# First group's maxima between the last projection products, and layer 1's projections mixed with base and adapter products, in a two-layer transformer kernel

## The reference, cut to what matters

```python
x = L0_attn_x                                   # (2, 1024, 512) f32
xn = _layernorm(x)
x = x + attn0(xn) + ffn0(xn)                    # 32 heads of 16, one k/v head, biases; SwiGLU 512 -> 1376
xn = _layernorm(x)
x = x + attn1(xn) + ffn1(xn)                    # 32 heads, 8 k/v heads, rotary, causal; base + routed adapters
# attn:  Q, K, V = xn @ Wq, xn @ Wk, xn @ Wv ;  softmax(Q K^T / 4) V @ Wo
# ffn1:  xn @ W_base.T + b_base + 2 * sum over the top 2 of 8 experts of gate * (xn @ A_e.T) @ B_e.T   (rank 16)
```

## Time and profile before

| | us |
|---|---|
| median of 3 runs | 2045.32 (2042.33 to 2059.11) |
| the profiled execution | 2046.85, of which its span is 2045.3 |
| layer 0: feed-forward, until | 389.9 |
| layer 0: 20 projection products | 389.9 to 461.5 |
| layer 0: group 0's 23 items alone | 464.3 to 492.8 |
| layer 0: attention and output | 492.8 to 1250 |
| layer 1: base and adapter products | 1274.0 to 1345.2 |
| layer 1: 20 projection products | 1346.1 to 1415 |
| layer 1: V products | 1414.8 to 1443.6 |
| layer 1: group 0's 33 items alone | 1444.4 to 1470.1 |

### The profile page before, as it was taken

One profiled execution on the slowest core, in us unless ns is written; L12 is line 12 of the kernel. 1 busy time (PEld: TensorE's weight loads), 2 busy tenths in 40 slices (PEclk: granted clock), 3 DMA queues, 4 the chain that ended last, 5 costly groups with the idle time before them and its releaser, 6 DMA issues.

```text
span 2045.3 us, 29252 instructions
## 1 busy us (share of the span) xinstructions
PE 1932.7 (94%) x10864; PEld 973.7 (48%) x10864; DVE 1405.1 (69%) x1879; ACT 1094.6 (54%) x2177; POOL 233.4 (11%) x606
## 2 busy tenths in 40 slices
PE   6999999998999999999999999997899999999998
PEld 5888887633333333333333357443433333333436
DVE  6554545328999999999988736369677777777643
ACT  3221211232887887878777743024176666767562
POOL 1000000000000100001000000000124334232230
PEclk9999999996999999999999999998699999999799
DMA  6010100141222112211121001014212121221102
GB/s 207 1 47 1 43 1 1 33 143 41 45 42 61 32 32 42 44 30 31 32 56 30 8 21 38 0 31 120 62 29 47 31 51 29 48 46 31 28 10 86
DMA packets 79212, 87.53 MB, mean 43 GB/s; under 512 B 19072, under 2 KB 52864, under 8 KB 79072
## 3 DMA queue, kind: packets, MB, share of 16 engines
q1 hardware_dynamic: 79072, 85.67, 16.8%
HBM read 55.20 MB, written 20.71 MB: 37 GB/s over the span
## 4 chain that ended last, share of the span: by engine, by line
PE 79%; DVE 9%; ACT 7%; issue 2%; SPq 1%; DMA 1%; POOL 0%; DVEq 0%; POOLq 0%
PE ps L1373 19%; PE ps L1403 11%; PE ps L1088 7%; PE ps L1089 7%; PE ps L1090 7%; ACT arena L738 6%; PE ps L1399 6%; PE ps L1320 6%; PE ps L1228 4%; PE ps L1326 4%; DVE arena L996 4%; PE ps L1182 3%; PE ps L1323 1%; PE ps L1258 1%; SPq L430 1%
## 5 line engine op out<-in xcount | busy, mean ns | idle before, releaser
L996 DVE TENSOR_REDUCE arena<-ps 128x1 f32<-128x1024 f32 (+7 forms) x1024 | 976.6, 987 | 204.6 <-PE ps L1323 123.7
L738 ACT ACTIVATE arena<-ps 128x512 f32<-128x512 f32 (+3 forms) x1792 | 869.1, 555 | 396.9 <-PE ps L1399 203.0
L1373 PE MATMUL ps<-arena 128*17 128x512 f32 (+3 forms) x3584 | 436.8, 560 | 0.4 <-POOL arena L561 0.4
L1326 PE MATMUL ps<-slots 48*128 48x512 f32 x1024 | 409.8, 477 | 9.8 <-DVE arena L996 8.5
L1403 PE MATMUL ps<-slots 50*128 50x512 f32 x1024 | 383.7, 454 | 22.8 <-ACT arena L738 13.9
L1403 PEld LDWEIGHTS ps<-slots 50*128 50x128 f32 x1024 | 170.8, 186 | 319.2 <-ACT arena L738 273.3
L1320 PE MATMUL ps<-slots 96*128 96x512 bf16 (+3 forms) x768 | 221.1, 345 | 24.9 <-DVE arena L996 13.1
L1399 PE MATMUL ps<-slots 98*128 98x512 bf16 (+3 forms) x768 | 218.3, 335 | 6.2 <-ACT arena L738 3.3
L1326 PEld LDWEIGHTS ps<-slots 48*128 48x128 f32 x1024 | 172.0, 191 | 58.5 <-DVE arena L996 33.5
L561 POOL TENSOR_SCALAR_AFFINE_SELECT arena<-arena 128x128 f32<-128x128 f32 x512 | 146.4, 293 | 382.9 <-ACT arena L738 371.8
L622 ACT ACTIVATE xn<-ps 128x512 f32<-128x512 f32 (+1 forms) x44 | 26.3, 598 | 259.6 <-PE ps L1090 259.6
(11 more groups left out here) (126 smaller groups left out, 1796.1 us busy)
## 6 DMA issues: line engine op xcount, KB each, us to landing
slots<-qparts SPq DMA_DIRECT2D x96, 128.0 KB, 3.6
qparts<-arena SPq DMA_DIRECT2D x32, 256.0 KB
xnT<-arena SPq DMA_DIRECT2D x256, 32.0 KB
slots<-qparts SPq DMA_DIRECT2D x96, 64.0 KB, 3.3
qparts<-arena SPq DMA_DIRECT2D x48, 128.0 KB
slots<-qparts SPq DMA_DIRECT2D x32, 192.0 KB, 3.7
w_raw<-in_wgu SPq DMA_DIRECT2D x20, 256.0 KB, 3.2
acc<-in_x SPq DMA_DIRECT2D x4, 1024.0 KB, 7.5
```

Of the source, the lines that this page charges most:

```text
L738: act.activation(prob[local % P_RING][:, q0:CH], bank(local % SP_RING)[:, q0:CH], ACT.Exp, scale=SCALE).then_inc(S["p_ready"], 1)
L996: dve.tensor_reduce(maxes[c][:, h * TPC + qt:h * TPC + qt + 1], src[:, 0:max_width(l == 1, c, qt)], AX_X, ALU.max).then_inc(S["x_done"], 1)
L1326: last = pe.matmul(dst[:, k0:k1], q_slot[u][r:r + ROWS[0], c, h % 2, qt * P:(qt + 1) * P].bitcast(F32R), k_slot[u][r:r + ROWS[0], k0:k1].b ...
L1373: mm = pe.matmul(bank(7)[32 * h:32 * h + DH + 1, q0:CH], v_slot[n % SLOTS][:, kt, :], prob[idx % P_RING][:, q0:CH], start=(kt == 0), stop= ...
```

## The change

Banks are given out anew in the projections: product i goes to bank i % 3, so banks 3 to 6 are free for items. `maxima_behind(l, i, count)` says which of group 0's items are issued behind product i: in layer 0 three behind each from product 12 on (two behind the last), in layer 1 six behind each from product 14 on (three behind the last). DVE's order has the same: behind its own step for product i stand those items' reductions. In layer 1 the weights and buffers of ffn1 move to other addresses, products 0 to 9 are issued between the base and adapter products (which keep banks 3 to 6; the transposes of the adapter input and the V products all use bank 7), and each of products 10 to 19 is followed by one or two V products. SP issues `load_ffn1` later (after the last output product of layer 0), writes group 0's first maximum rows behind `store_parts(l, 1)`, ahead of the load of slot 1, and no longer behind it.

```diff
+HWT_RING = 8
+ROPE_AT = {0: 0, 1: 1, 2: 2, 3: 3, 4: 4, 5: 5, 7: 6, 9: 7, 12: 8, 15: 9}
+PRODUCT_AT = {2: 5, 4: 6, 7: 7, 10: 8, 13: 9}
+FIRST_MAX_AT = [12, 14]
+MAX_PER_PRODUCT = [3, 6]
...
+def maxima_behind(l, i, count):
+
+    lo = max(0, i - FIRST_MAX_AT[l]) * MAX_PER_PRODUCT[l]
+    hi = max(0, i + 1 - FIRST_MAX_AT[l]) * MAX_PER_PRODUCT[l]
+    return (min(lo, count), count if i == NCH * (KC + 1) - 1 else min(hi, count))
+
+
+def values_behind(i):
+
+    first = QC * (KC + 1)
+    return [(max(0, j - first) + max(0, j - first - 4)) for j in (i, i + 1)]
...
-                sp.wait_ge(S["v_slot_ready"], SLOTS)
+                sp.wait_ge(S["v_slot_ready"], 1)
                 load_slot(l, 0)
                 store_parts(l, 1)
+                max_rows(l, 0, 0, 0)
+                sp.wait_ge(S["v_slot_ready"], SLOTS)
                 for n in range(1, SLOTS - 1):
                     load_slot(l, n)
                 for m in range(NQ):
                     sp.wait_ge(S["q_out"][m], 16 * PARTS[l] * NCH)
-                max_rows(l, 0, 0, 0)
...
+                if l:
+                    for t in range(TT):
+                        if t in ROPE_AT:
+                            roped(ROPE_AT[t])
+                        base_evac(t)
+                    for i in range(QC * NQ, NCH * NQ):
+                        roped(i)
+                        done = first_maxima(i, done)
+                    for i in range(NCH * NQ, NCH * NQ + HI_LAG + 1):
+                        roped(i)
+                else:
+                    for i in range(NCH * NQ):
+                        lower(i)
+                        if i >= NQ and i % NQ == 0:
+                            take_v(i // NQ - 1)
+                        done = first_maxima(i, done)
+                    take_v(NCH - 1)
...
+                def first_maxima(i):
+
+                    lo, hi = maxima_behind(l, i, min(cut(0), len(blocks[0])))
+                    for piece in first:
+                        if lo <= piece[0] < hi:
+                            if piece[0] == 0 and piece[5] == 0:
+                                pe.wait_ge(S["slot_in"][0], 16 * 12)
+                                pe.wait_ge(*((S["b_evac"], TT) if l else (S["y_evac"], TT * len(ROUNDS) + 1)))
+                            max_piece(*piece)
+
+                if l == 0:
+                    for i in range(NCH * NQ):
+                        product(i)
+                        if i >= NQ and i % NQ == 0:
+                            transpose_v(i // NQ - 1)
+                        first_maxima(i)
+                    transpose_v(NCH - 1)
+                else:
+                    pe.wait_ge(S["wf_in"], 16 * 2)
+                    for i in range(3):
+                        product(i)
+                        base_product(i)
+                    for i in range(3, NQ):
+                        product(i)
+                    transpose_hw(0)
+                    for t in range(TT):
+                        if t < TT - 1:
+                            transpose_hw(t + 1)
+                        lora_product(t)
+                        if t < TT - 3:
+                            base_product(t + 3)
+                        if t in PRODUCT_AT:
+                            product(PRODUCT_AT[t])
+                    for i in range(QC * NQ, NCH * NQ):
+                        product(i)
+                        for t in range(*values_behind(i)):
+                            value_product(t)
+                        first_maxima(i)
```

More of the change, by code:

```diff
@@ L674, in middle, with whole @@
                     act.activation(part1[m][:, 1, :], rest[m], ACT.Copy).then_inc(S["mid_done"], 1)
-                for i in range(NCH * NQ):
+                def whole(i):
                     c, m = divmod(i, NQ)
-                    rows = 2 * DH if (m == KC and l == 0) else P
                     if c:
@@ L692, in _ @@
[L692 to L698, removed]
+                        high(i, src, bias if m < KC else bias_kv[0:DH, 0:1])
+                        act.activation(q32[m][0:rows, :], src[0:rows, :], ACT.Identity, bias=bias).then_inc(S["q32_ready"], 1)
+                    else:
+                        act.activation(q32[m], src, ACT.Copy).then_inc(S["q32_ready"], 1)
@@ L966, in lowest @@
                     dve.tensor_tensor(part1[m][:, 2, :], rest[m], part1[m][:, 1, :], ALU.subtract).then_inc(S["lo_done"], 1)
[L968 to L984, removed]
-                    take_v(NCH - 1)
                 def maximum(j, n, c, qt, h):
@@ L1009, in maximum, with base_evac, roped, first_maxima @@
                     dve.sem_inc(S["x_done"], 1)
+                def base_evac(t):
+                    dve.wait_ge(S["b_ready"], t + 1)
+                    dve.tensor_tensor(acc[:, t, :], acc[:, t, :], bank(3 + t % 4), ALU.add).then_inc(S["b_evac"], 1)
+                def roped(i):
+                    if i < NCH * NQ:
+                        rope(i)
+                    if HI_LAG <= i < NCH * NQ + HI_LAG:
+                        remainder(i - HI_LAG)
+                    if i > HI_LAG:
+                        lowest(i - HI_LAG - 1)
+                first = max_blocks()[0]
+                count = first.index((0, 0, None, None)) + AHEAD[l] - 1
+                done = 0
+                def first_maxima(i, done):
+                    for j in range(*maxima_behind(l, i, min(count, len(first)))):
+                        maximum(j, *first[j])
+                        done += 1
+                    return done
+                if l:
+                    for t in range(TT):
+                        if t in ROPE_AT:
+                            roped(ROPE_AT[t])
[3 more added lines that the diff above has]
+                        done = first_maxima(i, done)
+                    for i in range(NCH * NQ, NCH * NQ + HI_LAG + 1):
+                        roped(i)
[6 more added lines that the diff above has]
+                    take_v(NCH - 1)
                 def invert(c0, c1, groups):
@@ L1020, in _ @@
                         invert(0, QC, NG)
-                    for item in block_:
+                    for item in block_[done if n == 0 else 0:]:
                         maximum(done, *item)
@@ L1233, in _ @@
-                if l == 0:
-                    transpose_v(NCH - 1)
-                for t in range(TT if l else 0):
-                    if t >= 3:
-                        pe.wait_ge(S["v_done"], t - 2)
-                    for k in range(KC):
-                        last = pe.matmul(bank(5 + t % 3)[:, 0:kw], xnT[:, k, t * P:(t + 1) * P], w_kv[:, k, kw:2 * kw],
-                                         start=(k == 0), stop=(k == KC - 1))
-                    last.then_inc(S["v_ready"], 1)
-                pe.wait_ge(S["v_done"], V_STEPS[l])
@@ new lines, in value_product, with product @@
+                def value_product(t):
+                    pe.wait_ge(*((S["v_done"], t) if t else (S["hwT_sb"], TT)))
+                    for k in range(KC):
+                        last = pe.matmul(bank(7)[:, 0:kw], xnT[:, k, t * P:(t + 1) * P], w_kv[:, k, kw:2 * kw],
+                                         start=(k == 0), stop=(k == KC - 1))
+                    last.then_inc(S["v_ready"], 1)
+                def product(i):
+                    c, m = divmod(i, NQ)
+                    if i >= 3:
+                        pe.wait_ge(S["q32_ready"], i - 2)
+                    for k in range(KC):
+                        wide = P if m < KC or l else 2 * kw
+                        w = w_q[:, k, m * P:(m + 1) * P] if m < KC else w_kv[:, k, 0:wide]
+                        last = pe.matmul(bank(i % 3)[0:wide, :], w, xnT[:, k, c * CH:(c + 1) * CH],
+                                         start=(k == 0), stop=(k == KC - 1))
+                    last.then_inc(S["q_ready"], 1)
```

148 lines of the change are left out of this document (72 added, 76 removed).

## The result

The changed kernel takes 2080.25 us, median of 4 runs (2076.57 to 2082.75), against 2044.13 (2042.33 to 2059.11): a ratio of 1.0166, 95% interval 1.0133 to 1.0200. The forecast was 2079. The profiled execution took 2076.57, its span is 2075.1, 29.8 longer than before.

A forecast was written before the change was run, and what follows sets the result against it. DVE was taken as the bound of layer 0's stretch and as falling behind PE in layer 1. Profiled 2046.9 + 5.4 (layer 0) + 19.3 (layer 1) + 9.3 (clock) = 2080.9, median 1.5 below: 2079 us, range 2055 to 2096.

The forecast's parts named there:

- Layer 0's turns: Layer 0: PE and DVE alternate, seven gaps of 4.1 us, 7.5 behind product 19; in sum +5.4 us.
- Layer 0's clock: Layer 0: no loss to half clock in the gaps of 4.1 us, taken as 0, with 13 us kept for a rival.
- rival B: Layer 0: every gap sends PE to half clock, products 13 to 19 start there, +13 us, 2092 in all; chance 0.17.
- Layer 1's first half at nothing: Layer 1: ten products more, 34.3 us, PE free at 1379.3; DVE's work on products 0 to 9 hidden, no extra cost.
- Slot 0's wait: Layer 1: slot 0 there at 1409.8, PE at the first item about 1402, so it waits 8 us.
- The series: Layer 1: product, DVE's step and reductions follow one another, 48.2 us behind products 15 to 18; second half +19.3 with slot 0.
- Layer 1's clock: Layer 1: products 15 to 19 each start at half clock, 5 x 1.85 = +9.3 us.
- C: Rival, both layers: reductions done while PE works, layer 0 -13.5 us, layer 1 -3, 2029 in all; chance 0.08.

The follow-up runs named there:

- e2: The changed kernel with DVE, in layer 1 alone, making each gap's reductions before it rotates and splits the product just ended: 2072.16 us, ratio 1.0154.
- e7: The changed kernel with layer 1's maxima starting behind product 16 in place of 14, nine in each gap in place of six: 2072.00 us, ratio 1.0114.
- e8: The changed kernel with three matmuls of unused result (2.8 us) in each gap ahead of the third item: 2072.67 us, ratio 1.0145.
- e3: The changed kernel with DVE, in both layers, making each gap's reductions before it splits the product just ended: 2058.31 us, ratio 1.0064.

## Why the prediction was right

**Layer 0's turns** were right: gaps of 4.07 against 4.1; the end from product 19 leaving PE (498.0) to the first score 7.6 against 7.5.

**Layer 0's clock** was wrong. The step that failed is the 0 I took for the gaps of 4.1 us, keeping 13 for rival B. Products 13, 14, 16 and 18 ran 5.3 or 5.4 where 3.6 to 3.7 is the full-clock length, about 1.65 more each: 4 x 1.65 = 6.6, and 5.4 + 6.6 = 12.0 against 11.9 measured. Rival B was half true: its price for one product, 1.85, was near, and not every gap sends the clock down. Nor are four of seven and these four a fixed pattern: the same code of layer 0 had products 13, 15 and 17 at half clock in e2, and 13, 14, 15, 17 and 19 in e7. In e8, with work in the wait, none started there. The Trainium skill ("TensorE: Matmul & The Clock Gate", HAM oscillation) describes such an oscillation, with every burst behind a wait starting cold; the trace agrees for three to five of the seven gaps of layer 0 and not for the others.

**Layer 1's first half at nothing** was right: product 10 starts 106.1 behind layer 1's first instruction, where 105.3 was forecast (1379.3 less 1273.96).

**Slot 0's wait** was right: forecast 1409.8, found 1421.62, which is 1409.7 without the 11.9 of layer 0. PE's idle time is 6.34 against 8. e7, which removes it and two gaps with it, gains 8 to 9, not the 19 I expected there.

**The series** of product, step and reductions was right: products 15 to 19 start within 54.1, where 48.2 + 4 x 1.85 = 55.6 was forecast, and it is 31.6 from product 19 to the mark against 30.5 + 1.85.

**Layer 1's clock** was a little dear: by the chain the five products took 5.85, 4.45, 5.20, 4.86 and 4.38, 7.5 more than 5 x 3.45, where 9.3 stood. L1 is 26.8 longer against 19.3 + 9.3 = 28.6.

So L0 and L1 sum to 38.7 against 34.0 forecast. The median lies 36.1 above before and 1.3 above the forecast: that it came so near owes something to chance. The sum started from the profiled execution of the kernel before, which has the half-clock stretch of the tail, and the profile after doesn't have it: 38.7 longer in L0 and L1, 8.9 shorter behind them, 2076.57 where 2080.9 was forecast for it. And medians of one kernel taken at different times differ by some us. What decides C, whether DVE may reduce before it splits, was the right question: e3 makes C's order, and gets 22 us back, though not the 50 that C priced. In layer 0, C took a gap to be the third item's matmuls alone, 1.4; PE still waits 1.31 for the first reduction, and the gap is 2.7. In layer 1, C left out the wait for slot 0: the first item starts 135.8 behind layer 1's first instruction in e3 as after. And the end behind product 19 is longer with this order, 33.9 against 31.6.

## What to carry to other kernels

Work moved into the gaps of another engine is free only if the engine that consumes it isn't the one that hands the other its next operand: write down, for one step, who waits for whom, and if DVE's order has its old duty first, product and new work take turns. Look at what stands behind the last step too: deferring a splitting or a store lengthens the end chain and gives back part of what it saved in the gaps (here 2.2 of 14.1 and 2.6 of 9.5 us). An interleaving and a move made together should be timed apart: here one gave 6 us and the other cost 42.

## What the runs showed of the hardware that I had not expected

Gaps of about 4 us with some 1.4 us of matmuls in them sent TensorE to half clock in four of seven steps (5.3, 5.3, 3.7, 5.4, 3.7, 5.4, 3.6 for products 13 to 19), in three and in five in other profiles of the same code; with 2.8 us of unused matmuls in each all seven products ran at full clock, and the median was 7.6 us lower. And half clock came too where PE was 99% busy (1075 to 1100 in e3), without anything of the change nearby, and what sets it off no run shows. The same kernel at a mean clock of 0.963 takes 15 to 20 us more than at 0.974, about half of the effect studied. A single profile can carry 7 to 12 us of that.
